# Two expert layers around an attention layer: ScalarE scales the last gathered rows of the first layer, eight scatter transfers are no longer held, the last block is added in halves

## The reference, cut to what matters

```python
x = x + 0.5 * ffn(layernorm(x))     # 14 routed experts, top 2 of them, and 2 shared experts
x = x + attention(layernorm(x))     # 16 heads of 8, causal, with a bias by key position
x = x + 0.5 * ffn(layernorm(x))     # the same experts again
```

## Time and profile before

| what | us |
|---|---|
| median of three runs | 1014.22 |
| lowest and highest of the three | 1011.94, 1020.28 |
| the profiled execution's own time | 1006.91 |
| its span, first to last instruction | 1005.0 |
| TensorE matmul busy | 915.0 |
| VectorE busy | 659.6 |
| ScalarE busy | 509.7 |
| GpSimd busy | 386.5 |

### The profile page before, as it was taken

One profiled execution on the slowest core, in us unless ns is written; L12 is line 12 of the kernel. 1 busy time (PEld: TensorE's weight loads), 2 busy tenths in 40 slices (PEclk: granted clock), 3 DMA queues, 4 the chain that ended last, 5 costly groups with the idle time before them and its releaser, 6 DMA issues.

```text
span 1005.0 us, 19516 instructions
## 1 busy us (share of the span) xinstructions
PE 915.0 (91%) x6961; PEld 566.9 (56%) x6961; DVE 659.6 (66%) x1697; ACT 509.7 (51%) x826; POOL 386.5 (38%) x447
## 2 busy tenths in 40 slices
PE   5798979888897999999999999999999888969996
PEld 4576979762443444544444445444453347969864
DVE  5856325558695688797788877887868547324422
ACT  2333646440264566556655565665556654636531
POOL 4375655463671500002201005007500465564564
PEclk9979989995798999999999999999999997979998
DMA  9712545355102231400423102304000013546432
GB/s 300 229 48 76 175 125 166 98 165 139 47 4 51 70 87 28 97 4 17 117 51 74 26 1 86 87 13 96 4 3 1 27 48 103 171 120 163 129 84 66
DMA packets 84260, 85.36 MB, mean 85 GB/s; under 512 B 11732, under 2 KB 73444, under 8 KB 81700
## 3 DMA queue, kind: packets, MB, share of 16 engines
q1 hardware_dynamic: 50842, 55.08, 20.6%
q0 software_dynamic: 8192, 16.79, 6.0%
q10 hardware_dynamic: 25132, 12.26, 4.1%
HBM read 52.48 MB, written 37.45 MB: 89 GB/s over the span
## 4 chain that ended last, share of the span: by engine, by line
PE 53%; DMA 19%; DVE 11%; issue 6%; POOL 5%; ACT 2%; DVEq 2%; POOLq 1%; SPq 0%
PE banks L1939 10%; PE banks L1909 9%; DMA region_c<-sorted_y,pos 9%; PE banks L1922 9%; PE banks L1831 6%; PE banks L1843 6%; DMA region_b<-sorted_y,pos 4%; DVE nmax L1493 3%; DMA sorted_x<-region_b,pos 2%; POOL sorted_x L824 2%; PE banks L1925 2%; PE banks L1912 2%; PE banks L1819 2%; PE banks L1703 1%; DVE nmax_late_keys L1493 1%
## 5 line engine op out<-in xcount | busy, mean ns | idle before, releaser
L1077 ACT ACTIVATE work<-banks 128x1024 f32<-128x1024 f32 (+3 forms) x384 | 300.4, 812 | 234.3 <-PE banks L1925 185.5
L1493 DVE TENSOR_REDUCE nmax<-banks 128x1 f32<-128x512 f32 (+3 forms) x432 | 271.7, 665 | 49.8 <-PE banks L1909 23.5
L1909 PE MATMUL banks<-ks,qs 75*128 75x512 bf16 (+3 forms) x576 | 183.3, 347 | 10.4 <-DVE nmax L1493 5.8
L824 POOL DMA_INDIRECT sorted_x<-region_b,pos x112 | 113.3, 1012 | 142.0 <-DVEq L1315 76.7
L1939 PE MATMUL banks<-work,vaug 128*9 128x512 f32 (+3 forms) x1536 | 161.3, 492 | 0.0
L1922 PE MATMUL banks<-qs,ks 78*128 78x512 bf16 (+3 forms) x576 | 154.3, 330 | 4.1 <-ACT work L1077 3.2
L1373 DVE COPY region_c<-w 128x512 f32 x184 | 73.2, 439 | 110.5 <-PE banks L1843 101.1
L1493 DVE TENSOR_REDUCE nmax_late_keys<-banks 128x1 f32<-128x384 f32 (+3 forms) x176 | 109.4, 638 | 43.2 <-PE banks L1912 38.5
L1909 PEld LDWEIGHTS banks<-ks,qs 75*128 75x128 bf16 x576 | 55.9, 99 | 136.4 <-DVE nmax L1493 71.5
L1831 PE MATMUL banks<-xTp,region_c 128*128 128x128 f32 x736 | 102.4, 284 | 3.0 <-ACT xTp L977 2.5
L1925 PE MATMUL banks<-identb,maskb 128*128 128x128 bf16 x512 | 103.3, 221 | 0.0
(11 more groups left out here) (212 smaller groups left out, 1172.5 us busy)
## 6 DMA issues: line engine op xcount, KB each, us to landing
xld<-sorted_x SPq DMA_DIRECT2D x92, 128.0 KB
sorted_y<-ysb ACTq DMA_DIRECT2D x92, 128.0 KB
qs<-q_scr SPq DMA_DIRECT2D x36, 192.0 KB
ks<-k_scr SPq DMA_DIRECT2D x36, 192.0 KB
q_scr<-qp SPq DMA_DIRECT2D x15, 256.0 KB
region_c<-q_scr SPq DMA_DIRECT2D x12, 192.0 KB
region_c<-k_scr SPq DMA_DIRECT2D x12, 192.0 KB
k_scr<-kp SPq DMA_DIRECT2D x9, 256.0 KB
```

The lines of the kernel that those rows point to most:

```text
L824: nc.gpsimd.indirect_dma_start(out=sorted_x[r], out_offset=bass.IndirectOffsetOnAxis(ap=pos[r][:, k, t:t + 1], axis=0), in_=xh_tile(f, r * ...
L1077: nc.scalar.activation(pT[s % 2][pair][:, :, 0:w], ps_s[pair][:, :, 0:w], ACT.Exp).then_inc(s_e, 1)
L1493: nc.vector.tensor_reduce(dst, ps_in_turn[SLOT["bank", u * NB + n]][:, 0:len(pieces) * w].rearrange("p (h j) -> p h j", j=w), axis=AXX, op ...
L1909: last = mm(dst, qs[g][0:PASS1_ROWS, h, it * P:(it + 1) * P], ks[g][0:PASS1_ROWS, h, j0:j0 + w], start=True, stop=not diagonal)
```

## The change

GpSimd's multiplications and VectorE's two fused parts in the first layer's second group go. ScalarE now multiplies all eight parts in place, six of them ahead of its first exp and the other two in steps 4 and 5. GpSimd adds all eight. The first eight scatters of a second group no longer wait in `keep_pace`. In the last layer parts 4 and 5 are added before `finish()`, and the last four tiles are added and stored two at a time.

```diff
+LAST_ROWS = 2
-DVE_PARTS = 2
-STEPS_ADD_AT = [4, 5]
+GATED_AHEAD = 6
+STEPS_GATED_AT = [4, 5]
+UNPACED = 8
...
-            sp.wait_ge(ffn[0].add, BLOCKS + DVE_PARTS // TOP_K)
+            sp.wait_ge(ffn[0].add, BLOCKS)
...
-            for t in range(0, TILES, BLOCK):
-                sp.wait_ge(ffn[1].add, t // BLOCK + 1)
+            stores = [(t, BLOCK) for t in range(0, TILES - BLOCK, BLOCK)]
+            stores += [(t, LAST_ROWS) for t in range(TILES - BLOCK, TILES, LAST_ROWS)]
+            for i, (t, n) in enumerate(stores):
+                sp.wait_ge(ffn[1].add, i + 1)
...
                 if r:
-                    pool.wait_ge(o.used, RING + SHARED_OF[f] + max(0, move - 8) // 2)
+                    if move >= UNPACED:
+                        pool.wait_ge(o.used, RING + SHARED_OF[f] + (move - UNPACED) // 2)
...
             def pool_adds():
 
                 pool.wait_ge(ffn[0].acc, CHUNKS)
-                for i in range(DVE_PARTS, TOP_K * BLOCKS):
+                for i in range(TOP_K * BLOCKS):
                     j, k = i // TOP_K, i % TOP_K
-                    for s, count in moved(MOVES * GATHERS[1] + TOP_K * BLOCK * j, TOP_K * BLOCK):
-                        pool.wait_ge(s, count)
-                    for t in range(BLOCK * j, BLOCK * (j + 1)):
-                        nc.gpsimd.tensor_scalar(got_rows(0, 1, k, t), got_rows(0, 1, k, t),
-                                                gates[1][:, k, t:t + 1], None, ALU.mult)
-                    pool.drain()
+                    pool.wait_ge(s_gated, i + 1)
...
+            def gate_part(i):
+
+                j, k = i // TOP_K, i % TOP_K
+                for s, count in moved(MOVES * GATHERS[1] + TOP_K * BLOCK * j, TOP_K * BLOCK):
+                    act.wait_ge(s, count)
+                for t in range(BLOCK * j, BLOCK * (j + 1)):
+                    rows = got_rows(0, 1, k, t)
+                    nc.scalar.activation(rows, rows, ACT.Copy, scale=gates[1][:, k, t:t + 1])
+                act.drain().then_inc(s_gated, 1)
...
+                    if span is FIRST_STEPS and s in STEPS_GATED_AT:
+                        gate_part(GATED_AHEAD + STEPS_GATED_AT.index(s))
...
             run_ffn(0, True)
+            act.wait_ge(s_gates, 1)
+            for i in range(GATED_AHEAD):
+                gate_part(i)
             steps(0, FIRST_STEPS, [])
...
+            def add_last(first):
+
+                for s, count in moved(MOVES * GATHERS[2 * GROUPS - 1] + TOP_K * first, TOP_K * LAST_ROWS):
+                    dve.wait_ge(s, count)
+                for k in range(TOP_K):
+                    dve.drain()
+                    for t in range(first, first + LAST_ROWS):
+                        rows = xs[:, GT + t, :]
+                        nc.vector.scalar_tensor_tensor(rows, got_rows(1, 1, k, t), gates[1][:, k, t:t + 1],
+                                                       rows, ALU.mult, ALU.add)
+                dve.drain().then_inc(ffn[1].add, 1)
...
+                for i in range(len(LATE_ADD_AT), TOP_K * (BLOCKS - 1)):
+                    add_part(f, 1, i)
                 finish()
                 if f:
-                    for i in range(len(LATE_ADD_AT), TOP_K * BLOCKS):
-                        add_part(f, 1, i)
+                    for t in range(GT - BLOCK, GT, LAST_ROWS):
+                        add_last(t)
...
-                    for i in range(DVE_PARTS):
-                        if span is FIRST_STEPS and s == STEPS_ADD_AT[i]:
-                            add_part(0, 1, i)
```

More of the change, by code:

```diff
@@ L507, in moved @@
                     for i in range(MOVE_SEMS) if any(n % MOVE_SEMS == i for n in range(first, first + count))]
+        s_gates = sem("last_rows_gates_made")
+        s_gated = sem("last_rows_part_gated")
         s_padd = sem("last_rows_added_by_pool")
@@ L699, in _ @@
             pairs(1)
-            for t in range(0, TILES, BLOCK):
-                sp.wait_ge(ffn[1].add, t // BLOCK + 1)
+            stores = [(t, BLOCK) for t in range(0, TILES - BLOCK, BLOCK)]
+            stores += [(t, LAST_ROWS) for t in range(TILES - BLOCK, TILES, LAST_ROWS)]
+            for i, (t, n) in enumerate(stores):
+                sp.wait_ge(ffn[1].add, i + 1)
                 sp.wait_ge(ffn[1].acc, t // CT + 1)
-                sp.dma_start(out[:, t:t + BLOCK, :], xs[:, t:t + BLOCK, :]).then_inc(s_out, 16)
-            sp.wait_ge(s_out, 16 * (TILES // BLOCK))
+                sp.dma_start(out[:, t:t + n, :], xs[:, t:t + n, :]).then_inc(s_out, 16)
+            sp.wait_ge(s_out, 16 * len(stores))
         @block.gpsimd
@@ L1343, in place @@
                                                 ALU.mult)
+                        if f == 0 and r == 1:
+                            dve.drain().then_inc(s_gates, 1)
                 return choose, place, choose_half, choose_tiles
```

## The result

The changed kernel took 1006.68 us (median of 20 runs, 1001.47 to 1013.09), the kernel before 1014.81 us in its 20 runs beside them. The ratio is 0.9925, with a 95% interval of 0.9903 to 0.9947: 7.6 us faster. The ratio comes from the single runs and not from the two medians, which lie 8.1 us apart; so do the ratios of the experiments. That is a real gain, less than the 1% bound of the prediction and less than its 10.8 us. The time lies in the range. The profiled execution took 1001.86 us with a span of 1000.1, so that the profiled pair shows only 4.9 us of span.

The account below looks back on a forecast made before the run. TensorE was taken to carry most of the chain, with GpSimd holding it in two first-layer stretches. The terms summed as 5.2 + 3.7 + 1.9 = 10.8 us off 1014.2, so 1003.4 us; range 994 to 1012.

Parts of the forecast that it names:

- the scatter is hidden anyway: Rival, turn of the groups: idle piece not the scatter's, group 0's rows bind; sum -6.6, 1007.6 us; chance 0.08.
- Term one: First layer's turn from group 0 to 1: eight scatters not held bring the first gather earlier, -5.2 us.
- the first step that failed: Second group's scatter: 31 steps keep 1.60 us each, so the last scatter goes out at 134.9 instead of 141.21.
- The second failed step: First gather of the turn: it can go at 143.4 instead of 148.65, 5.2 us earlier.
- third step: From the turn until attention: all that follows hangs on these gathers or on TensorE, which gained more.
- Term two: Start of attention: ScalarE scales, GpSimd adds, VectorE reaches the normed rows at 305.1 instead of 307.3 and clock is kept; -3.7 us.
- The delay of the exp: First exp of attention: late by gather 23, two scaled parts and the table load, 4.2 us, bounds 2.1 and 6.5.
- the 2.3 us that VectorE was spared: Start of attention: VectorE loses its two parts, 1.14 us each, and these count as it is nearly full.
- The clock kept behind the stall: Behind VectorE's former stall in attention: TensorE keeps its granted clock, 2.8 us at most, taken as 1.5.
- a wait takes the place of the stall: Rival, start of attention: ScalarE's delay and low clock, or late statistics, eat the gain; sum -7.1, 1007.1 us; chance 0.36.
- Term three: Kernel's end: parts 4 and 5 added in VectorE's idle time, last two tiles end at 1000.2 instead of 1002.2; -1.9 us.
- The first exp waits for gathers: Rival, start of attention: ScalarE's queue ties TensorE to gather 23, late gathers land on the path; 1016.8 us; chance 0.08.

Follow-up runs that it names:

- part one alone: Kernel before with only the first eight scatters of the second group not held, run on a second chip: 1009.30 us, ratio 0.9971.
- scatter again: Kernel before with the first eight moves of the second scatter not held and nothing else, on a second chip: 1009.30 us, ratio 0.9971.
- weights first: Changed kernel with VectorE's 14 scalings of the routed weights put ahead of a shared chunk: ratio 0.9935.
- never held: Changed kernel with no hold on any of the second group's scatters in the first layer: one run, 1007.95 us.
- scatter alone: Kernel before with only the first eight scatters of the second group not held, on a slower chip: 1060.13 us, no ratio formed.
- end alone: Kernel before with only the new end: parts 4 and 5 added earlier, last four tiles added and stored by twos: ratio 0.9979.
- drain often: Changed kernel with a GpSimd drain ahead of every fourth scatter and gather of the first layer: 1042.50 us, ratio 1.0275.
- no drain: Changed kernel without the GpSimd drain behind the memset, between last scatter and first gather: ratio 0.9964.
- four in flight: Changed kernel with four semaphores for the moves instead of two: 980.04 us, ratio 0.9672.

## Why the prediction was near and where it missed

**The chain at the turn of the groups** was read rightly. The idle piece of 5.35 us is attached to the scatter and not to group 0's stores (the rival *the scatter is hidden anyway*): it moved with the scatter, and no drain, no piece. That it is the drain alone was only guessed from a second place; the kernel without it showed this.

**Term one was mis-sized**, and this is the first step that failed: "The 31 steps from 91.52 to 141.21 took 1.60 us each; at that rate the last scatter goes out at 134.9". The rate was carried over as if it were GpSimd's own. It held 13.6 us of waits for landings, and with two moves in flight these grew to 16.7 us when moves 0 to 7 came earlier. The last scatter was at 138.6, beyond even the late bound of 137 (and the steps took 1.64 to 1.79 us in the five like kernels on these chips), so TensorE kept 3.9 of its 5.7 us of wait. The second failed step is the gather's: 143.4 was about the time at which group 0's rows are there (where a gather waited for them it went at 141.4 to 142.7), but the scatter with its drain came later, 146.2. At `norm(0)` 3.35 us were gained (181.39 against 184.74) where 5.2 were forecast.

A third step failed with it: "All that follows until attention hangs on these gathers or on TensorE, which gained more." The prediction counted as if the whole stretch moved by one amount. TensorE's side kept its 3.3 us until the exp. GpSimd's gathers, each waiting for the landing two back, lost most of theirs: the last one gained 0.9 us with part one alone and 1.1 in the whole change. The stall of VectorE, which ends with GpSimd, therefore grew when part one came alone, and 0.8 us of the gain were left.

**Term two**: the mechanism is right in each piece (no stall, GpSimd done early, the load behind six parts, clock kept). Its size is read from *scatter again*, which has part one and not part two. From there to the changed kernel the normed rows come 1.5 us earlier (304.97 against 306.47), and VectorE's next join of maxima (L1533, L1502 there) 3.0 us earlier (327.08 against 330.07). Forecast were 2.2 and 3.7, and the run of its own gives 3.3 with its wide interval. These are single traces: in *weights first* and *never held* the same join is at 328.8 and 327.5, so each number is uncertain by 1 to 2 us.

Two sizes inside the term were off. The delay of the exp was summed as 0.5 + 2.4 + 1.3 = 4.2 and measured 5.9: gather 23 landed at 261.7, 1.4 us behind the scores, and not 0.5; a part took 1.28 us with 0.14 to 0.45 between, not 1.2; the load was 1.28. And the 2.3 us that VectorE was spared shortened nothing. From its reduction some 14 us behind the exp to its normed rows VectorE took 24.3 us before, 24.6 in *scatter again* and takes 24.5 now. Behind that reduction, up to the next join of maxima, it now waits 2.65 us for TensorE's banks, and in both others 0.75. What made up for it is the stall, which was 6.60 and not 5.54 us once part one is in. The lower granted clock behind the exp is real, but it is no price of the change: over the 12.8 us behind the exp it is 0.74 now, 0.78 before and 0.68 in *scatter again*, and the way to that reduction was 14.3, 14.0 and 15.1 us.

The clock kept behind the stall is as forecast, 1.5 us. The stretch from the normed rows to the next join took 23.6 us in the two traces with stalls of 5.54 and 6.60 us, and 23.3 in the one with 6.10 (*scatter alone*). It takes 22.1 in the ten without a stall, and in *end alone*, with one of 2.60 us.

The rival *a wait takes the place of the stall* did not come, for VectorE has no wait there, though ScalarE's delay of 5.9 us ate most of the stall's 6.60. The measured 7.6 us are nearer to this rival's 7.1 than to the forecast's 10.8. That is chance: its 7.1 holds 5.2 us of term one and none of term two, while the runs show less of the one and most of the other.

**Term three** is right: 1.7 us by the pair, 1.1 to 2.6 over the traces, for 1.9.

The sum of the profiled pair up to the next join is 3.8 us: 0.8 that part one brings alone and 3.0 by part two on top. With 1.7 at the end it is 5.5, of which 0.6 are lost again between 327 us and the last layer's end (the shared chunk at 993.27 is 3.2 us earlier, not 3.8): the 4.9 of the spans. *The first exp waits for gathers* did not happen: gather 23 kept within 1.4 us of the scores. Of the six signs named for being right, the four of parts two and three came (no wait of VectorE for GpSimd, the load behind 24 copies, adds that end 19.3 us behind the last gather, the last addition 1.5 us behind its landing). The two of part one, TensorE's wait under 1 us and a first gather at 143.5, did not.

## What to carry to other kernels

When a queue is let go earlier, ask what each of its steps waits for at its present rate: a rate read from a trace is a property of the engine only where its waits are subtracted. Here the wait for the landing two moves back held the scatter and all gathers; one number (two semaphores to four) gave 2.7% alone, some 27 us, where three careful edits gave 8. A gain at one point of a queue is not a gain at its end either: ask what each later step waits for. Work moved to an idle engine has to be done before that engine's next duty on the path: cost it by that instruction's start, with a table load if the function set changes. Read what a part is worth from a kernel that has the others, not from the part alone: part one alone grew the stall that part two takes away.

## What the runs showed of the hardware

- A GpSimd drain behind indirect transfers has a price for each transfer since the drain before it. The idle gap behind the instruction that it follows is 0.14 us with none of them, 0.31 with 2 and 0.47 with 4 (drain often), 1.62 with 18, 3.91 with 46, 6.87 with 82 (no drain): (6.87 - 0.14) / 82 = (3.91 - 0.14) / 46 = (1.62 - 0.14) / 18 = 0.082 us. The 64 scatters give 5.25 us and the piece was 5.35. It does not lapse with time: `norm(0)` paid it for the 82 some 10 us behind the last of them. A drain that follows directly on a transfer takes 2.19 to 2.25 us in the second scatter and up to 4.99 among the gathers (drain often).
- ScalarE scales four 128x128 blocks by a column of gates in 1.26 to 1.28 us; GpSimd takes 2.34 to 2.46 for the same.
- A table load in front of an exp, behind a scaled copy, costs its 1.28 us and no more (the exp starts 1.44 us behind the copy's end with it, 0.16 without). Scaled copies run behind silu without a load.
- Indirect transfers from GpSimd are issued 1.25 to 1.46 us apart when nothing holds them (four in flight); with two in flight they came 1.60 (before) and 1.72 us apart (changed) in the second scatter. The Trainium skill, "DMA: Bandwidth & Descriptors", "Anatomy of one DMA — SWDGE (gpsimd) path", fits the duration of one as 2.0 us and its bytes over 436 KB a microsecond; a move here is 128 rows of 512 bytes, 65.5 KB, and an estimate by the page is 2.15 us. The chain of the changed kernel shows more, 2.49 to 2.88 for its six gathers between 244 and 262 us with two in flight, and 4.09 to 8.54 in crowded stretches. The measurement decides.
- The granted clock of TensorE was 0.87 to 0.88 over the stretch behind a stall of 5.54 to 6.60 us (three traces), and 1.00 where there was no stall or one of 2.60 (eleven). The same work took 23.3 to 23.6 us and 22.1 us.
